# Multiplying zeros on TensorE while a kernel's first weights are still being loaded

## The reference

```python
def attention(x):                       # x: 4 x 512 x 128
    q, k, v = x @ Wq, x @ Wk, x @ Wv    # 16 heads of 8
    gk = log_sigmoid(x @ Wgk1 @ Wgk2 + bgk2) / 16
    # for each token t: state = state * exp(gk_t) + v_t (outer) k_t ; out_t = state . q_t
    out = scan_over_tokens(q, k, v, gk)
    out = normalise(out) * gamma + beta
    return (out * silu(x @ Wg)) @ Wout

def ffn(x):                             # 128 -> 512 -> 512 -> 512 -> 128
    h = silu((x @ w1.T) * s1) * ((x @ w2.T) * s2)
    h = gelu((h @ h1.T) * sh1)
    h = gelu((h @ h2.T) * sh2)
    return (h @ w3.T) * s3

x = layernorm(x + attention(x))
return layernorm(x + ffn(x))
```

## Time and profile before

| what | value |
|---|---|
| median of 3 runs | 186.07 us (184.8, 186.07, 186.28) |
| the profiled execution: time / span | 184.29 us / 182.5 us |
| mean granted clock of TensorE in it | 0.996 |
| POOL busy | 113.1 us, 62% of the span |
| ACT busy | 111.6 us, 61% |
| PEld busy | 123.2 us, 68% |
| DMA | 8.97 MB, queues busy in the first 23 us |

### The profile page before, as it was taken

One profiled execution on the slowest core, in us unless ns is written; L12 is line 12 of the kernel. 1 busy time (PEld: TensorE's weight loads), 2 busy tenths in 40 slices (PEclk: granted clock), 3 DMA queues, 4 the chain that ended last, 5 costly groups with the idle time before them and its releaser, 6 DMA issues.

```text
span 182.5 us, 2765 instructions
## 1 busy us (share of the span) xinstructions
PE 161.6 (89%) x802; PEld 123.2 (68%) x802; DVE 148.0 (81%) x306; ACT 111.6 (61%) x179; POOL 113.1 (62%) x96
## 2 busy tenths in 40 slices
PE   0898988999879997999999699999996998999980
PEld 0755756868657774878778477577773885887770
DVE  1499989979889997998999997989999794874062
ACT  4554889992157453478683547667635669959421
POOL 8997898879609688670677678608685320670032
PEclk9999999999999999999999999999999999999998
DMA  3999900000000000000000001000000120000102
GB/s 115 313 389 416 381 18 0 0 4 0 4 0 0 2 0 0 4 2 0 0 0 0 0 0 57 0 0 0 4 0 0 48 83 0 4 0 0 57 4 63
DMA packets 6496, 8.97 MB, mean 49 GB/s; under 512 B 562, under 2 KB 5203, under 8 KB 5971
## 3 DMA queue, kind: packets, MB, share of 16 engines
q1 hardware_dynamic: 5906, 5.93, 10.2%
q0 software_dynamic: 576, 2.88, 4.1%
HBM read 7.76 MB, written 1.05 MB: 48 GB/s over the span
## 4 chain that ended last, share of the span: by engine, by line
PE 37%; DVE 13%; ACT 4%; issue 3%; POOL 3%; POOLq 0%; DVEq 0%
PE ffn L608 6%; PE ffn L617 6%; PE att L530 4%; PE ffn L586 2%; DVE y L1083 2%; PE att L655 2%; PE ffn L674 2%; PE att L643 2%; PE att L514 2%; DVE y L1087 2%; PE ffn L667 2%; PE ffn L591 2%; PE att L515 2%; DVE o_acc L1090 1%; PE att L541 1%
## 5 line engine op out<-in xcount | busy, mean ns | idle before, releaser
L1072 DVE TENSOR_TENSOR_SCAN state<-gate,att 128x512 f32<-128x512 f32 x32 | 38.3, 1208 | 1.5 <-PE att L530 1.5
L366 POOL TENSOR_TENSOR f_lo<-full,f_hi 128x512 fp32r<-128x512 f32 x18 | 23.4, 1315 | 25.9 <-DVE full L1158 18.2
L894 ACT ACTIVATE f_hi<-ffn,vec_cols 128x512 fp32r<-128x512 f32 x24 | 16.6, 690 | 25.1 <-PE ffn L617 24.9
L325 POOL TENSOR_TENSOR u_tok<-kv_tok 128x1024 f32<-128x1024 f32 (+1 forms) x12 | 27.3, 2281 | 1.9 <-DVE o_acc L1090 1.4
L608 PE MATMUL ffn<-f_hi,h_hi 128*128 128x512 f32 x96 | 27.3, 404 | 0.0
L617 PE MATMUL ffn<-f_lo,h_hi 128*128 128x512 f32 x96 | 26.6, 399 | 0.0
L340 POOL TENSOR_TENSOR o_acc<-o_acc,y 128x512 f32<-128x512 f32 x16 | 20.7, 1296 | 7.9 <-DVE y L1083 7.7
L1083 DVE TENSOR_TENSOR y<-att,state 128x512 f32<-128x512 f32 x32 | 21.1, 670 | 0.0
L608 PEld LDWEIGHTS ffn<-f_hi,h_hi 128*128 128x128 f32 x96 | 17.6, 188 | 4.7 <-ACT f_hi L886 0.9
L617 PEld LDWEIGHTS ffn<-f_lo,h_hi 128*128 128x128 f32 x96 | 17.8, 188 | 4.1
L530 PE MATMUL att<-ident,u_tok 128*128 128x128 f32 x128 | 18.5, 275 | 1.3 <-DVE u_tok L1049 0.9
(11 more groups left out here) (176 smaller groups left out, 357.9 us busy)
## 6 DMA issues: line engine op xcount, KB each, us to landing
h_raw<-in_hT SPq DMA_DIRECT2D x2, 1024.0 KB, 12.5
h_hi<-in_hT POOLq DMA_DIRECT2D x2, 1024.0 KB, 11.9
x_tok<-in_x SPq DMA_DIRECT2D x4, 256.0 KB, 5.8
out<-out_tok SPq DMA_DIRECT2D x3, 256.0 KB, 2.3
w_raw<-in_w12T SPq DMA_DIRECT2D x1, 512.0 KB, 5.5
w_hi<-in_w12T POOLq DMA_DIRECT2D x1, 512.0 KB, 8.8
xT_raw<-in_xT SPq DMA_DIRECT2D x1, 256.0 KB, 2.7
proj_raw<-in_proj SPq DMA_DIRECT2D x2, 128.0 KB, 2.3
```

The costliest lines, as they stand in the source:

```text
L325: nc.gpsimd.tensor_tensor(u_tok[:, j].rearrange("p k (h v) -> p k h v", v=DH), v_b.unsqueeze(1).to_broadcast([P, DH, HEADS, DH]), k_b.unsq ...
L366: nc.gpsimd.tensor_tensor(lo[:, o], full_block(layer, o), hi[:, o].bitcast(F32), ALU.subtract).then_inc(pool_rested, 1)
L894: nc.scalar.activation(hidden[layer][0][:, o], bank[:], ACT.Gelu, scale=scales[:, 1 + layer, o:o + 1]).then_inc(gelu_hi_ready, 1)
L1072: nc.vector.tensor_tensor_scan(state[:, k % 3], gate[:, b], A[2 + k % 2][:], 0.0, ALU.mult, ALU.add).then_inc(scanned, 1)
```

## The change

PE gets a wait for a new semaphore and four float32 matmuls ahead of its wait for `gk_loaded`. Their stationary operand is a 128x128 block of `u_tok`, their moving operand 256 columns of it, and they write to bank `F[3]`, whose content nobody reads before it is written anew. A fifth such matmul with 128 columns comes after L771. DVE sets the 256 columns of `u_tok` to zero ahead of its first wait. Nothing is removed.

```diff
+        warm_zeros = sem("warm_zeros")
...
+            zeros = u_tok[:, 0, 0:2].rearrange("p k c -> p (k c)")
+            pe.wait_ge(warm_zeros, 1)
+            for _ in range(4):
+                nc.tensor.matmul(F[3][:, 0:2 * P], u_tok[:, 0, 0], zeros, start=True, stop=True)
             pe.wait_ge(gk_loaded, 48)
             nc.tensor.matmul(A[3][:, P:2 * P], wgk1T[:], wgk2[:], start=True, stop=True).then_inc(gk12_ready, 1)
+            nc.tensor.matmul(F[3][:, 0:P], u_tok[:, 0, 0], u_tok[:, 0, 0], start=True, stop=True)
             project_kv(0)
...
             dve.sem_inc(yT_ready, 1)
+            nc.vector.memset(u_tok[:, 0, 0:2], 0.0).then_inc(warm_zeros, 1)
             rest_of_x(0)
```

## The result

The changed kernel takes 186.16 us at the median of 22 executions (185.37 to 188.53), the kernel before 184.99 us in as many beside them: ratio 1.0047, 95% interval 1.0025 to 1.0069. It is slower by some 0.9 us by the ratio and 1.17 us by the medians: inside the predicted range, but a real loss where a gain of 0.15 us was forecast. Ratios here leave out executions more than 1.5% above the fastest of their kernel; medians hold all.

What follows compares the result with a forecast made beforehand. The path was taken to be POOL and DVE alternating on the outer products behind the first k/v copy, then DVE without gaps. A gain of 0.15 us (between 0 and 0.5) off the 186.07 median gave 185.9 us, range 184.0 to 187.8.

Steps and rivals of the forecast that it cites:

- (1): DVE's memset of 256 columns ahead of its first wait: 0.31 us from about 0.95, PE starting near 1.4.
- Step (2): Four zero matmuls ahead of L771: 0.86 us each, 3.44 in all, overrunning the weights' arrival at 4.26 by 0.58.
- (3): ACT's roundings behind L771: L771 0.58 us later, ACT free at 7.38 against 6.80, still before 7.47.
- Step (4): 128-column zeros behind L771: 0.43 us, PE free at 5.70 before project_kv's wait ends at 5.81; cost 0.
- a sign against the forecast: Stages behind 40 us changing their length would show the forecast wrong, since nothing in them is touched.
- the forecast: Whole kernel: small gain of 0.15 us, clock holds, 185.9 us; chance 0.42.
- Step (5): Copies of k and v with an early clock: first copy gains 0.09, up to 0.5; 0.15 us taken.
- the exchange: POOL and DVE alternating on four outer products behind the k/v copies, 8.14 to 14.43; the path, starting with the first copy.
- rival D: Outer products behind the k/v copies don't take turns; second copy's 0.8 us passes on: 185.2 us; chance 0.04.
- Rival A: PE idles 4.2 us before the transposes of u, the clock falls, scan stage starts slow: +1.3, 187.4 us; chance 0.27.
- B: Clock rises early and stays, so all runs look like the profiled one: 184.1 us; chance 0.16.
- C: Zeros don't raise the clock in time (186.1), or a late memset delays L771 and project_kv (+0.3, 186.4); chance 0.11.

Runs made afterwards that it cites:

- three zeros with fillers: Changed kernel with three zero matmuls, none behind L771, plus six unread matmuls in PE's idle stretch ahead of the transposes of u: 185.28 us, ratio 0.9998.

## Why the prediction was wrong, point by point

The memset and PE's start (1) came as told: 0.27 us, 1.48. Step (2) was mis-sized: a pass of 256 columns takes 0.46 us, not 0.43, and L771 comes at 5.19, not 4.84 (0.08 by the start, 0.27 by the passes); hence ACT is free at 7.6 to 7.7 (3), not 7.38, past the old 7.47. **Step (4) failed**: "cost 0, with 0.11 to spare". L771 and the zeros behind it take 1.17 us, with 0.72 for L771, whose 128 columns I had put at 0.43 although show 0.79 for its two passes. So PE is free at 6.36, not 5.70, against a cover that ends at 5.81: the k and v products are 0.55 us late, and with them the first copy and the scans. Dropping the tail brings 0.41 us back in executions at a high clock, dropping the fourth matmul as well puts scan(0,2) at 20.16.

**A term that the sum doesn't have** is the memset's second price: DVE's two stops at 79 and 115 us, 0.3 us, in every kernel with that one memset. I had written that nothing behind 40 us is touched and named a change there as a sign against the forecast; it is there.

**The number was close by luck.** 186.16 lies 0.3 us from 185.9, but the forecast stood on a median of three, 186.07, where 22 executions give 184.99. The change itself was forecast at -0.15 us and came out at +0.9 by the ratio.

**Step (5) failed in its bound.** I let the gain reach 0.5 us with the first copy and said that the exchange starts with it. POOL can't start before its loads are issued, at 8.06. So, with POOL first in the turns, 0.08 us was all there was to win (the transposes of u come at 14.42 to 14.62 in the traces with an early clock, for 14.49), and I had left POOL's queue out of the sum. The turns of the earlier trace rows hold (rival D is dead: DVE ready at 8.13 gained nothing), but their order isn't fixed: in the trace with DVE ready at 8.13 POOL's second product goes ahead of DVE's first, in the earlier trace rows behind it.

**Rival A was right as a mechanism and too low as a chance** (0.27). Four of seven traces of the changed kernel show it, and 15 of 22 executions have a low clock against 35 of 93 (in other series). I took the hole at 4.2 us; it is 4.1 to 4.4. The price of 1.3 us against the kernel before is what three of the four traces show (1.37 to 1.47), and the fourth, 3.18, is near my figure for a slow clock all the way (2.9). My error was to treat A and the forecast as alternatives, when they are kinds of execution that mix, so that a share of A moves the median for certain. **B** may hold in half: slow executions at a high mean clock, which could be those that rise late, nearly vanish (11 of 58 against 1 of 28), but what replaces them is A. **C**'s second half, a late L771 that holds project_kv, is what happened in every slow-paced start, by overlong passes and not by a late memset, and at 0.55 us in place of 0.3.

Shown: the delay (0.55 us) and DVE's stops (0.3), together 0.85 in the trace and 0.73 between the high-clock medians; and the fall behind the idle stretch. Not settled: how the 0.9 us of the ratio divides between them, since the kernel before has low mean clocks too, some may be falls elsewhere, and no trace shows it in such an execution. Why DVE stops is open as well.

## What to carry to other kernels

Warming an engine is worth what the next consumer can take: follow the early result through each queue, DMA issues too, to the first instruction that starts earlier. Work that an early clock finishes sooner becomes idleness ahead of the next wait, and if the clock falls there the slow stretch moves to where it costs. An added instruction can also cost where nobody looks, 75 us later and on another path: compare two traces to their end. Size a filler to end before what it covers, with the measured duration of a pass, and put it where PE is idle late, not where it is idle first.

## What the runs showed of the hardware

Zeros alone can raise the clock: products at 0.12 us a step from 5.8 us on, behind nothing but zeros and L771, in three of the seven traces of the changed kernel and in one of three zeros with fillers; in the five traces without warming matmuls the first fast step comes at 8.6 us or later. The same program shows its first fast matmuls anywhere between 5 and 15 us. Idleness of 1.74 us kept the clock in one execution and 1.76 us lowered it in another; 2.4 to 4.4 us ahead of the transposes of u lowered it in six traces, while the twelve others, with 1.2 us or less there, kept it. The granted clock reads 1.00 ahead of its first change although the pace is half: only the steps between matmuls tell.
